# Seeding the penalty of a gather-by-product into PSUM, in a graph network on one core

## What is computed

```
W = (edge_attr @ ew + eb).reshape(E, 16, 16)
msg = einsum('ei,eio->eo', x[src], W)
agg = segment_sum(msg, dst, num_segments=N)
h = agg + x @ rw + rb
```

## Time and profile before

| | |
|---|---|
| median of 3 runs | 10,953.86 us (10,949.11 to 10,955.05) |
| span of the profiled execution | 10,954.1 us |
| granted TensorE clock, mean | 0.962; 1.00 inside the edge stages after the first |
| conv stages 2 and 3, with fill and drain | 2,532 us each |
| last edge stage | 2,388 us |
| busy: TensorE, ScalarE, VectorE, GpSimd | 88%, 64%, 60%, 73% |

### The profile page before, as it was taken

The page is one execution under the profiler, slowest core; times in us unless marked ns, Lnnn a source line. Parts: engine busy times, 40 slices in busy tenths (PEclk is TensorE's granted clock), DMA queues, the critical chain, the costliest instruction groups (busy, mean ns, idle before and its releaser), DMA issues.

```text
span 10954.1 us, 169268 instructions
## 1 busy us (share of the span) xinstructions
PE 9673.8 (88%) x49910; PEld 8173.9 (75%) x49910; DVE 6582.2 (60%) x10016; ACT 7059.5 (64%) x7283; POOL 8026.2 (73%) x8404
## 2 busy tenths in 40 slices
PE   5999999997199999999949999999993999999994
PEld 4888888886188888888838888888883888888883
DVE  6767676766266767677737676767673444444442
ACT  3676767675167677777726767676762677777762
POOL 6777777777577777777757777777775777777776
PEclk8999999998599999999979999999996999999997
DMA  4333333333133333333323333333331222222221
GB/s 112 110 106 111 111 110 106 111 111 93 43 106 111 109 107 111 111 107 109 110 64 111 105 112 110 110 106 111 111 104 35 55 55 55 59 58 55 55 55 26
DMA packets 430013, 1000.58 MB, mean 91 GB/s; under 512 B 168672, under 2 KB 268225, under 8 KB 397976
## 3 DMA queue, kind: packets, MB, share of 16 engines
q0 software_dynamic: 268800, 464.14, 18.3%
q1 hardware_dynamic: 161176, 536.02, 14.4%
HBM read 869.94 MB, written 129.62 MB: 91 GB/s over the span
## 4 chain that ended last, share of the span: by engine, by line
POOL 52%; issue 27%; DVE 10%; DMA 8%; PE 1%; DVEq 1%; SPq 0%; POOLq 0%; ACT 0%; ACTq 0%
POOL gathered L517 51%; DVE msg L903 7%; DMA gathered<-conv_table,idx 7%; DVE xe L821 1%; PE pY L434 1%; DVE idx L944 1%; DVEq L211 1%; SPq L231 0%; POOL gathered L1047 0%; PE pY L688 0%; DVE gathered L246 0%; DVE tmp L246 0%; DMA gathered<-in_dst,idx 0%; DMA gathered<-scanned,idx 0%; DMA conv_table<-gathered 0%
## 5 line engine op out<-in xcount | busy, mean ns | idle before, releaser
L688 PE MATMUL pY<-part,hot_key 128*128 128x400 f32 x40672 | 8624.4, 362 | 476.5 <-DVE xe L821 447.9
L688 PEld LDWEIGHTS pY<-part,hot_key 128*128 128x128 f32 x40672 | 7324.8, 189 | 757.2 <-DVE xe L821 593.0
L517 POOL DMA_INDIRECT gathered<-conv_table,idx x5952 | 5641.4, 948 | 2030.8 <-issue 1811.5
L821 DVE TENSOR_REDUCE xe<-pY 128x16 f32<-128x400 f32 x5084 | 2835.2, 567 | 1354.1 <-PE pY L690 1337.0
L568 ACT ACTIVATE apart<-key_pair,zone_lane 128x1408 f16<-128x1408 f16 x1984 | 2804.4, 1461 | 664.6 <-PE pY L690 639.5
L573 ACT ACTIVATE hot_key<-apart 128x1408 fp32r<-128x1408 f16 x1984 | 2612.0, 1365 | 0.0
L517 POOL DMA_INDIRECT gathered<-max_table,idx x1860 | 1812.2, 974 | 610.4 <-issue 566.5
L246 DVE TENSOR_TENSOR gathered<-gathered,pT 128x2048 f32<-128x2048 f32 x372 | 851.2, 2288 | 1512.8 <-DMA gathered<-conv_table,idx 1512.8
L690 PE MATMUL pY<-near_mask,not_near 128*128 128x400 bf16 x5084 | 1744.7, 343 | 0.0
L903 DVE TENSOR_REDUCE msg<-gathered 128x256 f32<-128x2304 f32 x744 | 1559.1, 2096 | 0.2
L690 PEld LDWEIGHTS pY<-near_mask,not_near 128*128 128x128 bf16 x5084 | 488.3, 96 | 898.8 <-issue 898.8
(11 more groups left out here) (122 smaller groups left out, 1812.6 us busy)
## 6 DMA issues: line engine op xcount, KB each, us to landing
key_pair<-key_rows SPq DMA_DIRECT2D x248, 1408.0 KB
scanned<-run_pair SPq DMA_DIRECT2D x248, 416.0 KB, 2.5
gathered<-conv_table,idx POOLq DMA_INDIRECT x5952
attr_pair<-in_attr SPq DMA_DIRECT2D x186, 208.0 KB
gathered<-max_table,idx POOLq DMA_INDIRECT x1860
conv_table<-gathered SPq DMA_DIRECT2D x24, 504.0 KB, 3.4
conv_table<-rows SPq DMA_DIRECT2D x18, 504.0 KB, 3.2
gathered<-scanned,idx POOLq DMA_INDIRECT x392, 2.3
```

What stands on the lines that cost most here:

```text
L517: e.indirect_dma_start(out=G[s][:, t, 0:width], out_offset=None, in_=table[:, :], in_offset=bass.IndirectOffsetOnAxis(ap=idx[s][:, t:t + 1 ...
L688: e.matmul(pG[bank], hot_key[s][:, z, at:at + P], part[:, z * NEAR:(z + 1) * NEAR, :], start=(z == 0 and k == 0), stop=False)
L821: e.tensor_reduce(xe[s][:, j * D:(j + 1) * D], pG[j % BANKS].rearrange("p (r d) -> p d r", d=D), AX.X, ALU.max).then_inc(s_pick.sem, 1)
```

## The change

- **No ninth product.** Before a step the bank is *seeded*: ScalarE (`act_seed`) writes |near - r| x 2^90 for the 25 candidates r into the bank, VectorE (`dve_seed`) does so in the last stage. The eight products are then added to it (`start=False`), and the pick is a minimum. Four products at the start of a stage (`pe_prime`) make the banks ready to be added to. `not_near`, its keys and their loads go.
- **Columns.** TensorE takes 11 of 26 (12 in the last stage), GpSimd 15 (14). The lots are 5 and 6 columns.
- **Zones.** In a convolution VectorE makes the fourth one-hot zone with one compare (`zone_compare`), at the top of `body`; ScalarE makes three. In the last stage ScalarE makes all four.
- **Order.** ScalarE's list is mixed anew (`conv_body`, `max_body`). On VectorE the attribute product is cut in two and the picks move. A column's bank is now its running number modulo 4, so loops are unrolled over 4 chunks in a convolution.

```diff
-TP_CONV, TP_MAX = 10, 11
+TP_CONV, TP_MAX = 11, 12
-LOTS = ((0, TH), (TH, TP_CONV))
+LOTS = ((0, 5), (5, TP_CONV))
...
             def pe_step(e, c, j):
...
+                gate(e, "pe", s_seed, at(c, tp, b_seed + j + 1))
                 for z in range(ZONES):
                     for k, part in enumerate(parts):
...
+                        ins = e.matmul(bank_of(c, j), hot_key[s][:, z, lanes_of],
+                                       part[:, z * NEAR:(z + 1) * NEAR, :], start=False,
+                                       stop=(z == ZONES - 1 and k == 1), skip_group_check=True)
-                e.matmul(pG[bank], not_near[s][:, at:at + P], near_mask[:, :, :],
-                         start=False, stop=True).then_inc(s_gath.sem, 1)
+                ins.then_inc(s_gath.sem, 1)
...
+            def act_seed(e, c, j):
+
+                if c[2] * tp + j >= BANKS:
+                    gate(e, "act", s_pick, at(c, tp, b_pick + j + 1 - BANKS))
+                e.activation(bank_of(c, j).rearrange("p (r d) -> p r d", d=D),
+                             far_ramp[:, :].unsqueeze(2).to_broadcast([P, NEAR, D]), ACT.Abs,
+                             bias=far_near[:, bass.ds(at(c, TP_KEYS, TP_KEYS - tp + j), 1)], scale=-1.0
+                             ).then_inc(s_seed.sem, 1)
...
+            def dve_seed(e, c, j):
...
+                e.tensor_scalar(bank_of(c, j).rearrange("p (r d) -> p r d", d=D),
+                                far_ramp[:, :].unsqueeze(2).to_broadcast([P, NEAR, D]),
+                                far_near[:, bass.ds(at(c, TP_KEYS, TP_KEYS - tp + j), 1)], FAR,
+                                ALU.not_equal, ALU.mult).then_inc(s_seed.sem, 1)
...
+            def zone_compare(e, c):
...
+                gate(e, "dve", keyed, pair_at(c, 16, 16))
+                gate(e, "dve", s_gath, at(later(c, -SLOTS), tp, tp + b_gath))
+                tt(e, hot_key[s][:, ZONES - 1, w], keys[s][:, w], last_zone[:, 0:1].to_broadcast([P, tp * P]),
+                   ALU.is_equal).then_inc(s_zone[s].sem, 1)
...
+                def follow(cp, j):
+
+                    ahead = j + BANKS - 1
+                    if ahead < tp:
+                        dve_seed(e, cp, ahead)
+                    elif again:
+                        dve_seed(e, later(cp, 1), ahead - tp)
```

`follow` puts the seed of column j + 3 behind the pick of column j, in the last stage. VectorE's new head of `body` in a convolution:

```diff
+                if again and not is_max:
+                    zone_compare(e, c2)
+                    next_picks(2)
...
+                    attrs(0, 8)
+                    if not again:
+                        next_picks(2)
+                    next_picks(3)
+                    m_g = attrs(8, tg)
+                    next_picks(4)
```

More of the change, by code:

```diff
@@ L1 @@
+import math
 import numpy as np
@@ L576, in hots_begin, with at @@
[L576 to L587, removed]
+        def at(c, mul, plus):
+            v, step_, n0 = c
+            return v * (step_ * mul) + (n0 * mul + plus)
@@ new lines, in pair_at, with later, slot, each_chunk @@
+        def pair_at(c, mul, plus):
+            v, step_, n0 = c
+            return v * (step_ // SLOTS * mul) + (n0 // SLOTS * mul + plus)
+        def later(c, k):
+            v, step_, n0 = c
+            return (v, step_, n0 + k)
+        def slot(c):
+            return c[2] % SLOTS
+        def each_chunk(e, lo, hi, turns, one):
+            lead = (hi - lo) % turns
+            for n in range(lo, lo + lead):
+                one((0, turns, n))
+            with e.Fori(0, (hi - lo) // turns) as q:
+                for m in range(turns):
+                    one((q, turns, lo + lead + m))
@@ new lines, in load_keys, with abs_zone @@
+        def load_keys(e, keyed, n, tp):
+            first_key = (TP_KEYS - tp) * P
+            e.dma_start(key_pair[:, :, first_key:PE_EDGES],
+                        key_pairs[bass.ds(n, 1), :, first_key:PE_EDGES].to_broadcast([P, SLOTS, tp * P])
+                        ).then_inc(keyed.sem, 16)
+        def abs_zone(e, s, z, k, tp, done):
+            gate(e, "act", s_abs, done)
+            w = slice((TP_KEYS - tp) * P, PE_EDGES)
+            e.activation(apart[k][:, w], keys[s][:, w], ACT.Abs, bias=zone_lane[:, z:z + 1]).then_inc(s_abs.sem, 1)
@@ L589, in first_keys, with relu_zone @@
+        def relu_zone(e, s, z, k, tp, done):
+            gate(e, "act", s_abs, done)
+            w = slice((TP_KEYS - tp) * P, PE_EDGES)
+            return e.activation(hot_key[s][:, z, w], apart[k][:, w], ACT.Relu, bias=1.0, scale=-1.0)
+        def first_keys(name, tp):
             keyed = sem(f"s_keyed_{name}")
-            b_hotk = [c.n for c in s_hotk]
+            b_hotk, b_zone = [c.n for c in s_hotk], [c.n for c in s_zone]
             def load(n):
@@ L617, in edges @@
             tg = T - tp
+            turns = math.lcm(BANKS // math.gcd(tp, BANKS), SLOTS)
             iters = CHUNKS // SLOTS
-            first, last = (0, 0), (iters - 1, 1)
-            b_free, b_run, b_hotk = ([c.n for c in cs] for cs in (s_free, s_run, s_hotk))
+            first, last = (0, turns, 0), (0, turns, CHUNKS - 1)
+            b_free, b_run, b_hotk, b_zone = ([c.n for c in cs] for cs in (s_free, s_run, s_hotk, s_zone))
             b_rf = s_runfree.n
@@ L703, in pe_product, with pe_body @@
                     return
[L705 to L710, removed]
+                gate(e, "pe", s_xeT, at(c, 2, half + 1 + b_xeT))
+                gate(e, "pe", s_multiplied, at(c, 2, half + b_mul))
+                a, b = LOTS[half]
+                for q, (k, m) in enumerate(PIECES[half]):
+                    ins = e.matmul(pE[:, q, 0:m * ROW], xeT[0:(b - a) * D, :],
+                                   edge_w[0:(b - a) * D, k * ROW:(k + m) * ROW], start=True, stop=True)
                 ins.then_inc(s_prod.sem, 1)
             def pe_hots(e, c):
-                gate(e, "pe", s_hotk[c[1]], c[0] + (b_hotk[c[1]] + 1))
-            def pe_body(e, c1, c2):
+                gate(e, "pe", s_hotk[slot(c)], pair_at(c, 1, b_hotk[slot(c)] + 1))
+                if not is_max and c[2] >= SLOTS:
+                    gate(e, "pe", s_zone[slot(c)], pair_at(c, 1, b_zone[slot(c)]))
+            def pe_body(e, c1, more):
+                c2 = later(c1, 1)
                 for j in range(HEAD, HEAD + 4):
@@ L724, in pe_body @@
                     pe_step(e, c1, j)
-                if c2 is not None:
+                if more:
                     pe_hots(e, c2)
@@ L742, in pe @@
                 pe_hots(e, first)
+                pe_prime(e)
                 for j in range(HEAD):
                     pe_step(e, first, j)
[L745 to L749, removed]
-            on("tensor")(pe)
-            def act_turn(e, c, half):
-                if is_max:
[L755 to L759, removed]
@@ L805, in act @@
+            act_body = max_body if is_max else conv_body
             def act(e):
                 e.wait_ge(s_init.sem, INIT_ALL + is_max)
[L807 to L813 removed]
+                if not is_max:
+                    e.wait_ge(s_primed.sem, primed)
+                    for j in range(8):
+                        act_seed(e, first, j)
+                act_body(e, first, False, True, True)
+                act_body(e, later(first, 1), True, True, True)
+                each_chunk(e, SLOTS, CHUNKS - SLOTS, turns, lambda c: act_body(e, c, True, True, True))
+                act_body(e, later(last, -1), True, True, False)
+                act_body(e, last, True, False, False)
@@ L930, in body @@
                                      ALU.max if is_max else ALU.add).then_inc(s_scan[s].sem, 1)
-                next_picks(7, 8)
-                if not is_max and c1 is not None:
-                    lot_product(e, c1, 0)
-                next_picks(*range(9, tp))
+                if is_max:
+                    next_picks(*range(7, tp))
+                else:
+                    next_picks(9)
+                    if more:
+                        lot_product(e, c1, 0)
+                    next_picks(10)
                 head_picks(0, 1)
-                gate(e, "dve", s_scan[s], i + (b_scan[s] + 1))
+                gate(e, "dve", s_scan[s], pair_at(c, 1, b_scan[s] + 1))
                 assert marks[0] == MARKS
```

378 lines of the change are left out of this document (230 added, 148 removed).

## The result

The changed kernel takes 11,300.45 us (median of 4 runs, 11,298.0 to 11,304.5), the kernel before 10,954.28 (median of 4): ratio 1.0317, 95% interval 1.0304 to 1.0329. It is slower by 346 us; 11,270 was forecast.

The account below looks back on a forecast made before the run. GpSimd's gathers were taken to bound the kernel, with TensorE close behind. 10,954 + 477 (three convolutions) - 158 (last stage) = 11,273, given as 11,270 us; range 10,900 to 11,540.

Parts of the forecast that it names:

- The loop: Convolutions: a closed path, 12.43 us on ScalarE plus 9.28 for the rest, makes 21.7 us a chunk, against 20.28 before.
- the 1.3 that was given as a sign: Convolutions: TensorE's idle time before step 8 would be near 1.3 us, released by the seed.
- The seed: ScalarE, convolutions: one seed takes 0.60 us, 0.51 apart, worked out from other rows as no row showed one.
- Eight products: TensorE: a step of eight products takes 1.47 us, nine took 1.65, so the ninth costs 0.18 us.
- Costed at nothing: VectorE, convolutions: 16.7 us of work a chunk, off the closed path, with picks done over 2 us early.
- GpSimd would wait for indices: Convolutions, a sign in the profile after: GpSimd waiting for indices, or VectorE no longer for rows; no size given.
- Costed at 19.0 us a chunk: GpSimd, convolutions: 15 gathers instead of 16, 15 x 1.27 = 19.0 us a chunk with the hiccups.
- The stage: Each convolution: filling 23.6 us, 121 loops, 20 for the chunk without new zones, draining 21: 2690 us against 2531, +159.
- Rivals 1: Convolutions: faster, the loop being shorter than added up; break-even at 20.8 us a chunk, down to 10,694 us; chance 0.14.
- rival 2: Convolutions: VectorE enters the loop, with the compare at twice its price and late picks; 11,700 us; chance 0.09.
- The last stage: Last stage: 14 gathers for 15, 19.17 to 17.9 us a chunk if GpSimd still bounds, -158 us.
- Rival 3: Last stage: no gain, because pick, seed and scan in one queue starve TensorE; 11,430 us; chance 0.09.

Follow-up runs that it names:

- the fastest variant: Changed kernel with seed 8 ahead of the transpose copy, store and attribute copy before the last-column wait, scalar-lane zone compare: 10,424 us, ratio 0.9528.
- the copy that moved 162 us or 3 us by its place: Changed kernel plus one unread ScalarE copy a chunk: ahead of seed 7, 11,463 us (+162); ahead of the last-column wait, 11,303 us (+3).
- both moves: Changed kernel with ScalarE's seed 8 ahead of the transpose copy, and store and attribute copy before the last-column wait: 10,571 us, ratio 0.9659.

## Why the prediction was right

**The loop.** 21.7 us a chunk forecast, 21.62 measured; 12.43 of it on ScalarE, and 12.35 in the timeline (Abs at 4000.59 to the end of seed 7 at 4012.94); 9.28 for the rest, and 9.26 (4012.94 to the next Abs at 4022.20), so no errors cancel. Before step 8 TensorE's products wait 1.10 us, near the 1.3 that was given as a sign. The prediction did not find this in any share of busy time: ScalarE went from 64% to 67%. It came from asking, of each instruction that changed place, what it now stands behind.

**The seed.** 0.60 us was worked out from three other rows; 0.585 us measured, 0.52 apart for 0.51. The group of all seeds:

```profile
L791 ACT ACTIVATE pY<-far_ramp,far_near 128x400 f32<-128x400 f32 x4092 | 2369.0, 585 | 290.0 <-DVE xe L931 226.4
```

The Trainium skill's page "ScalarE: Activation LUTs", what ACT_TABLE_LOAD costs, gives 280 ns + 0.833 ns an element for an ACTIVATE with one bias value per partition as an operand, by which 400 elements take an estimated 0.61 us, and an overlap of 93 ns; the trace agrees but for 0.03 us (585 ns), and its slope of 0.84 ns between 416 and 1408 elements is the same.

**Eight products.** 1.46 to 1.47 us a step in every profile after, so the ninth cost 0.18 us as read in the earlier trace rows. TensorE's list without a wait, in the fastest variant, is 19.1 us. The estimate of 0.169 us for one product, by the formula for an isolated matmul on the Trainium skill's page "TensorE: Matmul & The Clock Gate", back-to-back issue gap, does not hold for these products, which take 0.183 us each.

**VectorE.** Costed at nothing, and rightly: it waits for the attribute copy 1.8 us a chunk, and pick and compare have gone into its idle time. That GpSimd would wait for indices came true (2.1 us a chunk).

**GpSimd.** Costed at 19.0 us a chunk, it needed 19.8: its 15 gathers are 18.71, and the one that begins within the zone compare is 1.1 us longer, which the prediction did not have. It did not matter under a loop of 21.6 us; with seed 8 moved, and with both moves, it did.

**The stage.** 2690 us forecast, 2690.5 measured in the second convolution. Rivals 1 and 2 fall with this; the copy that moved 162 us or 3 us by its place excludes rival 2 as a sum.

**The last stage, where a term was mis-sized.** I took 14 gathers at 1.278 us, -158 us. The gathers run from 8899.2 to 11,150.2 us, against 8425.6 to 10,803.3 before: -127. A chunk takes 18.15 us for 17.9. The row that I divided (1800 us by 1408) holds 1.25 us a gather and 0.46 us a chunk, the one long gather, and this second part does not go when one gather goes. But that is 0.03 us a chunk, 4 of the 31 us: 14 x 1.2475 + 0.46 is 17.9 too. The missing term is a pause of GpSimd. Once in eight chunks, 15 times in the stage, a gather starts 1.8 to 2.0 us after the last one instead of 0.30:

```profile
10063.32 0.94 POOL L526 DMA_INDIRECT gathered<-max_table,idx  x1 [1.82 <-issue]
```

That is 0.2 us a chunk, 24 us in all, and the last stage of the kernel before has not one. The prediction took its mean from that stage and so put the pause at nothing. The long gather came out 0.04 us longer besides. GpSimd's timeline around a scan:

```profile
10012.84 0.94 POOL L526 DMA_INDIRECT gathered<-max_table,idx  x1 [0.30 <-issue]
10014.09 1.32 POOL L526 DMA_INDIRECT gathered<-max_table,idx  x1 [0.30 <-issue]
```

One gather of each chunk is long, as before, and it begins within VectorE's scan (10,013.64 to 10,014.65). Rival 3 fell: VectorE seeds at 0.63 us and still waits 2.1 us a chunk for gathered rows (206.2 us in 99). The convolutions grew by 158, 159 and 161 us for 159 each, so the last stage accounts for the 30 us between 11,273 and the profiled span of 11,302.7.

## What to carry to other kernels

With hand-written orders on in-order engines, take the sum of each engine first, and then look for a closed path: from one wait through the lists of the engines back to the same wait a turn later. What an instruction costs is set by its place on that path (0.44 us or nothing for the same copy), so an instruction that others wait for goes ahead of one that itself waits, even if both are short. A mean scaled by a count holds only if nothing new appears at the new count: ask which part goes with the count, which with the loop, and look at other stages for what comes by another count, as GpSimd's pause does.

## What the runs showed that was not expected

**Which passes lengthen a gather, and when.** GpSimd's gather of 0.94 us becomes longer when it begins while certain passes of VectorE run. In the changed kernel all 74 long gathers between 4000 and 5600 us began within the zone compare (0.94 to 2.05 us on average), and each ended 0.81 to 0.83 us after the compare did:

```profile
4003.88 2.20 POOL L526 DMA_INDIRECT gathered<-conv_table,idx  x1 [0.30 <-issue]
```

```profile
4003.64 1.63 DVE L250 TENSOR_TENSOR hot_key<-key_pair,last_zone 128x1408 fp32r<-128x1408 f16 x1
```

To run beside such a pass is not enough. The scan of the same chunk started 0.05 us after a gather had, and the gather was not longer:

```profile
4018.20 0.94 POOL L526 DMA_INDIRECT gathered<-conv_table,idx  x1 [0.30 <-issue]
```

```profile
4018.25 1.01 DVE L1078 TENSOR_TENSOR_SCAN rows<-flags,msg 128x416 f32<-128x416 bf16 x1
```

So it goes in all 74 chunks there, and for the 55 gathers that had begun before the compare. In the last stage, from 9100 to 10,900 us, 99 gathers begin within the scan, and all 99 end 0.75 to 0.76 us after it. What a gather costs is thus set by where in the pass it begins, and that by the order of the lists: the gather that begins within the compare took 2.05 us in the changed kernel and 1.44 us with both moves.

Not every pass does it. 47 gathers of the first stretch began within an attribute product and 222 within a sum of up to 2.4 us, and none became long; the compare and the scan read two tensors from SBUF, the attribute products one from PSUM. The compare with a scalar lane reads one, runs in 0.95 us instead of 1.62, and lengthens a gather still. The Trainium skill's page "SBUF — State Buffer", who interferes with whom, says that a VectorE instruction with two SBUF inputs contends with a GpSimd instruction that reads SBUF, and that one in a two-port mode holds a port pair that the two engines share. Both cases agree with these runs; that the fast compare ran in such a mode is read from its time alone. The same section infers that a tensor_tensor instruction does not hold up the making of DMA descriptors. Here such a compare lengthened 74 of the 74 gathers that began within it, and the measurement decides. A form that takes neither port was not tried, so the port as the cause is argued and not shown.

**The pause.** GpSimd's pause of some 2 us comes after every 112 gathers: in the convolutions of the kernel before, each seventh chunk of 16 (17 times a stage), and in the last stage of the changed kernel, each eighth chunk of 14 (15 times, and so in every run with 14). The last stage of the kernel before and all three convolutions with both moves, with 15 gathers a chunk, have none. No run tells the cause.
